# Edge lookups of a graph-attention router: a table of 116 rows and 27 blocks with a mask in twelve more rows, and one maximum in place of a product and a sum

## The chip, the cores and the metric

One core of one Trainium2 chip runs the whole program as a single launch. TensorE (PE in the profile), VectorE (DVE), ScalarE (ACT), GpSimd (POOL) and SyncE (SP, which here only issues DMAs) each run their own instruction stream and meet through semaphores. The metric is device time in microseconds from one launch; lower is better.

## The reference

The input is a graph with 3125 nodes of 256 features. The last of its stages, the only one whose main loop is touched, is a mixture of four experts whose router is a graph attention over 65536 edges and 4 heads:

```python
h = (x_flat @ W_gat).reshape(M, HEADS, NUM_EXPERTS)          # 4 heads x 4 experts
a_src = (h * att_src).sum(-1); a_dst = (h * att_dst).sum(-1)
e = leaky_relu(a_src[src] + a_dst[dst], negative_slope=0.2)
e_max = segment_max(e, dst); ee = exp(e - e_max[dst])
denom = segment_sum(ee, dst)
agg = segment_sum(h[src] * (ee / denom[dst])[:, :, None], dst)
scores = layernorm(agg + b_gat).mean over heads; w = softmax(top 2 of scores)
out = x + sum over experts ei of g[ei] * (gelu(x @ W1[ei] + b1[ei]) @ W2[ei] + b2[ei])
```

For each edge the kernel needs eight numbers of its destination node (two per head: a_dst less a bound, and 0.2 a_dst less the same bound) and twenty numbers of its source node.

## The kernel before, in words

The stage (`stage_router_and_experts`, tag `g1_`, F1 hidden columns) walks over 128 supertiles of 512 edges (GSUP = 128, SUP = 4 tiles of 128 edges), and beside them runs the experts: `program` spreads 4 experts x 5 groups of nodes x 6 steps = 120 steps over the first 120 supertiles, and the last 8 have edge work alone. All engines follow the order in which the code is written.

For supertile n the work is this.

- POOL gathers the twenty numbers of each edge's source by four indirect DMAs (`gather`, L2190), once DVE has copied their indices (`indices`, L2510).
- SP fetches the row numbers of the 512 edges, the same for every partition (`load_part`, L2659), and DVE compares them with the partition's own number (`turn_rows`, L2214): `turned_hot`, [125 rows, 512 edges], one-hot by row. The second instruction of `turn_rows` (L2217) makes `at_block`, a one-hot over 25 blocks for each edge.
- PE multiplies (`look_up`, L2753 and L2754) that one-hot with a table of 125 rows x 25 blocks x 8 numbers, cut in a high and a low part (`d_hi`, `d_lo`). What comes out in `found` (PSUM) is, for each edge, all 25 blocks of its row: 200 columns.
- DVE picks the block (`pick`): a product of the 800 numbers of a partition with `at_block` (L2524), a sum over the blocks (L2527), then three small instructions for the logit (L2531, L2532, L2535).
- ACT makes the weights (`weights`, L2806 and L2808, with two table loads) for two supertiles at once, and a one-hot over 261 places (`row_hots`, L2207 and L2210).
- DVE multiplies the weighted rows out over 12 classes (`scattered`, L2569, 1920 numbers), and PE adds them with 16 matmuls (L2735) into two PSUM banks.

DVE's order in supertile n is `weighted`, `classes`, `high`, `indices` for n + 4, `turned` for n + 3, `rest_of`, `pick` for n + 2, `scattered` for n. PE's order in step n is the sums of n with an expert's output (L2715, L2717) and one or two hidden tiles (L2197) between them, and `look_up` of n + 4. `look_up` of n + 4 waits for `turned` of n + 4 and for the reading of `found` by `pick` of n + 3 (semaphore `picked`); the sums wait for `spread_ready` and `hot_ready`.

At the stage's start DVE makes the table in place (`weigh_edges`, L2591 to L2595, semaphore `cut`), and PE begins with `pe.wait_ge(s["cut"], 5)`, `look_up(0, 0)`, hidden tiles, and three more lookups before step 0. The row and block numbers of the edges are worked out at the program's very start (`numbers` in `stage_open`), as work that DVE does between other work, and stored in DRAM by ACT (L1344). `gdst` is a DRAM tensor of 3125 x 8 that was used only in a branch for far-spread logits, which is not entered here.

## Time and profile before

| | |
|---|---|
| median of 3 runs | 4336.94 us (4331.12 to 4337.73) |
| profiled execution, its own time | 4339.91 us |
| its span | 4338.1 us |
| busy: PE, DVE, ACT, POOL | 3800.2, 2983.7, 2016.3, 2146.7 us |
| granted TensorE clock over the span | 0.871 of full speed |
| last stage | from about 3436 us to the end |

Times in views of the trace count from the span's start. An engine's busy time is the union of its instructions' durations. Matmuls are pipelined: each one's duration reaches over the start of the next, so the distance between two starts is what a matmul costs PE.

### The profile page before, as it was taken

Reading aid. Unit: us, or ns where it says so; the run is one execution under the profiler, and the core shown is the slowest. Engines: PE = TensorE matmul, PEld = TensorE weight load, DVE = VectorE, ACT = ScalarE, POOL = GpSimd, SP = SyncE. Lnnn points to the kernel's source line nnn. Section 1 sums busy time; section 2 is a strip of 40 time slices with the busy share of each in tenths; the row PEclk is TensorE's granted clock in tenths of the full one; section 3 lists DMA queues with packets and bytes.
Section 4 is the critical chain, followed back from the end, with each engine's and each line's share of the span. In section 5 each row is a group of like instructions: output and inputs, shape, how many; then the busy total and the mean of one; then the engine's idle time right before and its main releaser. Section 6 shows DMA issues by size and latency. Waiting matters only on the chain. (4 is left out here: it accounts for less than half of the span.)

```text
span 4338.1 us, 87724 instructions
## 1 busy us (share of the span) xinstructions
PE 3800.2 (88%) x23737; PEld 3412.1 (79%) x23737; DVE 2983.7 (69%) x6878; ACT 2016.3 (46%) x4710; POOL 2146.7 (49%) x2102
## 2 busy tenths in 40 slices
PE   7899999999999997997999677777777599999993
PEld 6799999999999986997887666666666578888883
DVE  7799999999999987555333222333332389999997
ACT  3566666666666655776222000000000278888871
POOL 0455555555555530000000777777777177777781
PEclk9999999999999997998999556666665599999996
DMA  4566666666666640002444333333333223333225
GB/s 132 148 175 178 176 176 177 175 178 176 175 178 175 178 122 18 19 14 65 160 150 151 110 105 105 104 104 105 105 104 105 57 59 78 69 77 73 62 51 122
DMA packets 226996, 509.04 MB, mean 117 GB/s; under 512 B 51806, under 2 KB 94300, under 8 KB 220427
## 3 DMA queue, kind: packets, MB, share of 16 engines
q0 software_dynamic: 116736, 313.66, 26.1%
q1 hardware_dynamic: 106389, 187.30, 15.5%
q10 hardware_dynamic: 3679, 5.79, 0.4%
q8 instruction: 89, 1.46, 0.1%
q14 instruction: 103, 0.84, 0.1%
HBM read 434.08 MB, written 72.49 MB: 117 GB/s over the span
## 5 line engine op out<-in xcount | busy, mean ns | idle before, releaser
L685 POOL DMA_INDIRECT big<-table,e_idx x784 | 747.1, 953 | 887.6 <-DVE e_idx L721 649.1
L356 POOL DMA_INDIRECT big<-table,e_idx x784 | 767.3, 979 | 819.6 <-DVE e_idx L460 353.5
L703 PE MATMUL psum<-e_near_hot,big 128*128 128x64 f32 x3136 | 604.0, 373 | 279.2 <-issue 200.6
L703 PEld LDWEIGHTS psum<-e_near_hot,big 128*128 128x128 f32 x3136 | 581.5, 284 | 312.4 <-issue 237.6
L2190 POOL DMA_INDIRECT g_S<-gsrc,g_idx x512 | 614.2, 1200 | 194.5 <-issue 158.9
L468 DVE TENSOR_TENSOR big<-psum,big 128x512 f32<-128x512 f32 x784 | 539.1, 688 | 36.9 <-PE psum L375 26.5
L435 ACT ACTIVATE e_hT_hi<-psum 128x256 fp32r<-128x256 f32 x784 | 300.7, 384 | 552.7 <-PE psum L375 552.7
L748 DVE TENSOR_TENSOR big<-big,psum 128x128 f32 x196 | 56.5, 288 | 662.9 <-PE psum L703 546.3
L386 PE MATMUL psum<-e_w_hi,e_hT_hi 128*128 128x256 f32 x1568 | 507.0, 323 | 0.3 <-ACT psum L420 0.3
L386 PE MATMUL psum<-e_w_hi,e_hT_lo 128*128 128x256 f32 x1568 | 442.1, 282 | 0.0
L386 PE MATMUL psum<-e_w_lo,e_hT_hi 128*128 128x256 f32 x1568 | 438.8, 280 | 0.0
L403 PE MATMUL psum<-e_near_hot,e_msg 128*128 128x64 f32 x3136 | 436.4, 262 | 0.2 <-DVE e_msg L506 0.2
L403 PEld LDWEIGHTS psum<-e_near_hot,e_msg 128*128 128x128 f32 x3136 | 411.7, 191 | 0.3 <-DVE e_msg L506 0.3
L2735 PE MATMUL psum<-g_hot,g_spread 128*120 128x262 f32 x2048 | 344.3, 305 | 42.6 <-DVE g_spread L2569 36.1
L506 DVE TENSOR_TENSOR e_msg<-psum,e_gate 128x256 f32<-128x256 f32 x784 | 331.0, 422 | 59.4 <-ACT e_gate L442 33.5
L223 ACT ACTIVATE e_t_low<-e_t_low 128x626 f32<-128x626 f32 (+1 forms) x10 | 7.2, 725 | 778.8 <-DVE e_t_low L232 778.8
L2735 PEld LDWEIGHTS psum<-g_hot,g_spread 128*120 128x120 f32 x2048 | 281.4, 187 | 67.4 <-issue 53.0
L481 DVE SCALAR_TENSOR_TENSOR e_hT_lo<-psum,e_hT_hi 128x256 fp32r<-128x256 f32 x784 | 324.6, 414 | 0.0
L442 ACT ACTIVATE e_gate<-big 128x256 f32<-128x256 f32 x784 | 318.8, 407 | 0.0
L367 PE MATMUL psum<-e_wb_hi,e_attr_parts 128*128 128x512 f32 x784 | 312.5, 399 | 2.5 <-DVE e_attr_parts L474 2.5
L368 PE MATMUL psum<-e_wb_lo,e_attr_parts 128*128 128x512 f32 x784 | 311.7, 398 | 0.0
L375 PEld LDWEIGHTS psum<-ident,big 128*128 128x128 f32 x1568 | 208.8, 141 | 128.1 <-issue 21.3
(395 smaller groups left out, 8942.5 us busy)
## 6 DMA issues: line engine op xcount, KB each, us to landing
big<-in_attr_t SPq DMA_DIRECT2D x392, 128.0 KB
g_rest<-gpart SPq DMA_DIRECT2D x128, 256.0 KB
big<-table,e_idx POOLq DMA_INDIRECT x1568, 2.8
table<-C SPq DMA_DIRECT2D x26, 896.0 KB
table<-n_rows SPq DMA_DIRECT2D x24, 896.0 KB
experts<-g_region SPq DMA_DIRECT2D x15, 560.0 KB
g_S<-gsrc,g_idx POOLq DMA_INDIRECT x512
table<-big SPq DMA_DIRECT2D x25, 224.0 KB
```

What stands on the lines that cost most here:

```text
L356: pool.indirect_dma_start(G[:, j % 2, q, :], None, table, bass.IndirectOffsetOnAxis(idx[:, j, q:q + 1], 0)).then_inc(s[f"G_in{j % 2}{q}"], 16)
L367: pe.matmul(c.ps[u % 2], tile, wb_hi[:, :], start=True, stop=False)
L386: last = pe.matmul(c.ps[4 + u % 2][:, 0:D], x, y[:, b, :], start=False, stop=b == KB - 1 and x is lo, skip_group_check=True)
L403: last = pe.matmul(acc[:, b, :], msg[:, u % 2, b * 128:(b + 1) * 128], hot, start=q == 0 and (b == 0 or s is sems[1]), stop=q == SUP - 1, ...
L442: act.activation(gate[:, u % SLOTS, :], Z[:, u % SLOTS, D:2 * D], ACT.Sigmoid).then_inc(s["gate_ready"], 1)
L468: dve.tensor_tensor(Z[:, u % SLOTS, :], c.ps[u % 2], G[:, j % 2, q, :], ALU.add).then_inc(s["zs_ready"], 1)
L481: dve.scalar_tensor_tensor(out=hT_lo[:, u % SLOTS, :, :].rearrange("p b n -> p (b n)"), in0=c.ps[2 + u % 2][:, 0:KB * 128], scalar=0.0, in ...
L506: dve.tensor_tensor(msg[:, u % 2, :], c.ps[4 + u % 2][:, 0:D], gate[:, u % SLOTS, :], ALU.mult).then_inc(s["msg_ready"], 1)
L685: pool.indirect_dma_start(G[:, j % n, q, :], None, c.table1, bass.IndirectOffsetOnAxis(idx[:, j, q:q + 1], 0)).then_inc(s[f"G_in{j % n}"], 16)
L703: last = pe.matmul(acc[:, b, :], G[:, j % n, q, b * 128:(b + 1) * 128], onehot[:, q, :], start=q == 0 and (b == 0 or s is sems[1]), stop=q ...
L2190: pool.indirect_dma_start(S[:, j, q, :], None, c.gsrc, bass.IndirectOffsetOnAxis(idx[:, j, 0, q:q + 1], 0)).then_inc(w_in[j], 16)
L2735: last = pe.matmul(sums[half], spread[:, j, 2 * u + p, half * CLASSES // 2:(half + 1) * CLASSES // 2, :].rearrange("p k c -> p (k c)"), ho ...
```

## The change

The table gets 116 rows and 27 blocks (116 x 27 = 3132), and twelve more rows: three for the tens digit of the block number to base 9, nine for its units digit. In these rows stands 0 for the blocks that have this digit, and -2^100 for those that don't. The one-hot gets 128 rows: the row number for partitions 0 to 115, the tens digit for 116 to 118, the units digit for 119 to 127. So in what PE gives out, every block but the edge's own is very negative, and DVE takes the maximum over the 27 blocks straight from PSUM. `at_block`, the product and one wait are gone. The table is brought into its new shape by a way through DRAM: rows_d to `gdst` and back into `table`. The constants `digit` and `off_block` are made in an earlier stage (`block_mask`, 12 small DVE instructions ahead of `stage_relations`' loop), the digits of the edges in `stage_open` (two more `divide`, two more stores by ACT).

```diff
+LP, LB, LOW = 116, 27, 9
+BIG = 2.0 ** 100
...
-                for out, made_here in ((c.gpart, at_row[:, 1, :]), (c.gnum[:, 0, :], block_of[:, 0, :]), (c.gnum[:, 1, :], at_row[:, 0, :]),
+                for out, made_here in ((c.gpart[0], at_row[:, 1, :]), (c.gpart[1], node[:, 1, :]), (c.gpart[2], block_of[:, 1, :]), (c.gnum[:, 0, :], block_of[:, 0, :]), (c.gnum[:, 1, :], at_row[:, 0, :]),
...
-                    yield from divide(block_of, at_row, node, TP)
+                    yield from divide(block_of[:, 0, :], at_row[:, 0, :], node[:, 0, :], TP)
+                    yield from divide(block_of[:, 1, :], at_row[:, 1, :], node[:, 1, :], LP)
+                    yield from divide(node[:, 1, :], block_of[:, 1, :], block_of[:, 1, :], LOW)
...
-        def turn_rows(dve, n, j):
-            dve.tensor_scalar(turned_hot[0:TP, j % 2, :], part_in[0:TP, j % 2, :], c.row[0:TP, :], None,
+        def turn_rows(dve, j):
+            dve.tensor_scalar(turned_hot[:, j % 2, :], part_in[:, j % 2, :], c.digit[:, :], None,
                               ALU.is_equal).then_inc(s["turned_ready"], 1)
-            c.fence(dve)
-            dve.tensor_tensor(at_block[:, j, :, :], bc(c.iota[:, 0:NT], 1, SUP),
-                              bc(lo[:, bass.ds(n * SUP, SUP)], 2, NT), ALU.is_equal).then_inc(s["block_ready"], 1)
+        PART_ROWS = ((0, LP), (LP, LP + LB // LOW), (LP + LB // LOW, 128))
...
                 dve.wait_ge(s["looked_up"], n + 1 + 2)
-                dve.wait_ge(s["block_ready"], n + 1)
-                dve.tensor_tensor(chosen_rows, found[:, :, 0:NT * 2 * GH].rearrange("p q (c t) -> p q c t", t=NT),
-                                  bc(at_block[:, j, :, :], 2, 2 * GH), ALU.mult).then_inc(s["picked"], 1)
+                dve.tensor_reduce(picked[:, j % 2, :, :], found[:, :, 0:LB * 2 * GH].rearrange("p q (c t) -> p q c t", t=LB), AX.X,
+                                  ALU.max).then_inc(s["picked"], 1)
+                x, above, below = w[:, j % 2, :, :], picked[:, j % 2, :, 0:GH], picked[:, j % 2, :, GH:2 * GH]
                 dve.wait_ge(s["picked"], n + 1)
-                dve.tensor_reduce(picked[:, j % 2, :, :], chosen_rows, AX.X, ALU.add).then_inc(s["e_steps"], 1)
...
+            dve.wait_ge(table_in, 32)
+            cut(dve.tensor_tensor(by_column, by_column, bc(c.off_block[:, :], 1, 2 * GH), ALU.add))
             cut(dve.tensor_copy(high_part, by_column))
             cut(dve.tensor_tensor(low_part, by_column, high_part.bitcast(F32), ALU.subtract))
...
             def load_part(n, j):
                 if not (isinstance(n, int) and n < 2):
                     sp.wait_ge(s["turned_ready"], n - 1)
-                c.fence(sp)
-                sp.dma_start(part_in[:, j, :], c.gpart[bass.ds(n, 1), :].broadcast_to([128, SUP * 128])).then_inc(
-                    s[f"part_in{j}"], 16)
+                for kind, (a, b) in enumerate(PART_ROWS):
+                    c.fence(sp)
+                    sp.dma_start(part_in[a:b, j, :], c.gpart[kind, bass.ds(n, 1), :].broadcast_to([b - a, SUP * 128])).then_inc(
+                        s[f"part_in{j}"], 16)
...
+            sp.wait_ge(s["cut"], 3)
+            for a, b in ROWS:
+                sp.dma_start(gdst_v[a:b], rows_d[a:b, :, :]).then_inc(table_out, 16)
+            sp.wait_ge(table_out, 32)
+            sp.wait_ge(cleared, 1)
+            whole = LP * (LB - 1)
+            sp.dma_start(table[0:LP, 0:LB - 1, :], c.gdst[0:whole].rearrange("(t p) d -> p t d", p=LP)).then_inc(table_in, 16)
+            sp.dma_start(table[0:NODES - whole, LB - 1, :], c.gdst[whole:NODES]).then_inc(table_in, 16)
             for n in (2, 3, 4):
                 load_part(n, n % 2)
...
-                    out = found[:, q, 0:NT * 2 * GH]
-                    hot = turned_hot[0:TP, j, q * 128:(q + 1) * 128]
+                    out = found[:, q, 0:LB * 2 * GH]
+                    hot = turned_hot[:, j, q * 128:(q + 1) * 128]
...
-            pe.wait_ge(s["cut"], 5)
+            pe.wait_ge(s["cut"], 6)
             look_up(0, 0)
```

DVE's instructions in one supertile of the loop, from the second one-hot (L2217, written to `g_region`, where at_block lies) to the last step of `pick`; before (ISA and REGISTER_ALU rows are waits and register steps):

```order
L2217 TENSOR_TENSOR g_region<-iota,g_rest 128x100
L2553 ISA
L2554 TENSOR_TENSOR g_parts<-g_R,g_parts 128x4x20
L2522 REGISTER_ALU
L2524 TENSOR_TENSOR g_chosen_rows<-psum,g_region 128x800
L2527 TENSOR_REDUCE g_picked<-g_chosen_rows 128x32
L2529 ISA
L2530 ISA
L2531 TENSOR_TENSOR g_w<-g_S,g_picked 128x16
L2532 SCALAR_TENSOR_TENSOR g_picked<-g_S,g_picked 128x4x4
L2534 REGISTER_ALU
L2535 TENSOR_TENSOR g_w<-g_w,g_picked 128x16
```

And of the change, the same place, from the row one-hot (L2240) on, which before stood two rows ahead of L2217:

```order
L2240 TENSOR_SCALAR g_turned_hot<-g_rest,digit 128x512
L2577 ISA
L2578 TENSOR_TENSOR g_parts<-g_R,g_parts 128x4x20
L2549 REGISTER_ALU
L2550 TENSOR_REDUCE g_picked<-psum 128x32
L2553 REGISTER_ALU
L2554 ISA
L2555 TENSOR_TENSOR g_w<-g_S,g_picked 128x16
L2556 SCALAR_TENSOR_TENSOR g_picked<-g_S,g_picked 128x4x4
L2558 ISA
L2559 TENSOR_TENSOR g_w<-g_w,g_picked 128x16
```

Two instructions are gone, and the reduction now reads PSUM itself, and is what frees it.

SP's instructions at the start of the stage's main block, of the change (`g_rest` holds part_in, 512 row numbers for each partition; before, only one issue of 128x512 stood here for each supertile):

```order
L2716 DMA gdst<-g_rows_d 112x25x8
L2716 DMA gdst<-g_rows_d 13x25x8
L2720 DMA g_table<-gdst 116x26x8
L2721 DMA g_table<-gdst 109x8
L2686 DMA g_rest<-gpart 116x512
L2686 DMA g_rest<-gpart 3x512
L2686 DMA g_rest<-gpart 9x512
```

The four table DMAs stand ahead of the first row loads, the second two wait for the first two, and DVE's `table_in` and with it PE's first lookup wait behind them.

## Rows read from the trace of the kernel before

**Rows 1.** Page: span; part 1, busy time of each engine.

```profile
span 4338.1 us, 87724 instructions
...
PE 3800.2 (88%) x23737; PEld 3412.1 (79%) x23737; DVE 2983.7 (69%) x6878; ACT 2016.3 (46%) x4710; POOL 2146.7 (49%) x2102
```

**Rows 2.** Windows: length, busy time of PE, PEld, DVE, ACT, POOL, clock, DMA.

```profile
3496.00:4187.00 691.00, 668.91 (x4187) 592.27 (x4187) 663.70 (x1473) 587.75 (x1041) 545.47 (x451) 1.00 0.31 69
4187.00:4266.00 79.00, 57.67 (x349) 52.73 (x348) 69.23 (x149) 42.47 (x82) 46.92 (x39) 0.85 0.51 104
```

**Rows 3.** Source view of L2569: duration min/median/max, first and last start.

```profile
L2569 DVE TENSOR_TENSOR g_spread<-g_at_class,g_parts x128: 2157/2158/2200, 3489.0 to 4260.9; 128x1920 fp32r<-128x1920 f32 x128
```

**Rows 4.** Groups by line, 3500 to 4180 us: busy, mean of one, idle before.

```profile
L2190 POOL DMA_INDIRECT g_S<-gsrc,g_idx x445 | 538.3, 1210 | 143.7 <-issue 139.8 <-DVE g_idx L2510 3.9
L2735 PE MATMUL psum<-g_hot,g_spread 128*120 128x262 f32 x1780 | 296.9, 302 | 21.6 <-DVE g_spread L2569 16.2 <-issue 4.1
L2569 DVE TENSOR_TENSOR g_spread<-g_at_class,g_parts 128x1920 fp32r<-128x1920 f32 x112 | 241.7, 2158 | 2.1
...
L2527 DVE TENSOR_REDUCE g_picked<-g_chosen_rows 128x32 f32<-128x800 f32 x112 | 110.4, 986 | 3.9
L2524 DVE TENSOR_TENSOR g_chosen_rows<-psum,g_region 128x800 f32<-128x800 f32 x111 | 108.5, 977 | 0.0
```

**Rows 5.** Waits of PE, 3490 to 4187 us: total, times, longest.

```profile
PE psum L2735 <- DVE g_spread L2569: 19.4, 26, 2.7
```

**Rows 6.** Timeline of DVE in one supertile: start, length.

```profile
3803.33 0.24 DVE L2217 TENSOR_TENSOR g_region<-iota,g_rest 128x100 f32<-128x100 f32 x1
3803.50 0.24 DVE L2554 TENSOR_TENSOR g_parts<-g_R,g_parts 128x80 fp32r<-128x80 f32 x1
3803.66 0.98 DVE L2524 TENSOR_TENSOR g_chosen_rows<-psum,g_region 128x800 f32<-128x800 f32 x1
3804.67 0.99 DVE L2527 TENSOR_REDUCE g_picked<-g_chosen_rows 128x32 f32<-128x800 f32 x1
3805.80 0.17 DVE L2531 TENSOR_TENSOR g_w<-g_S,g_picked 128x16 f32<-128x16 f32 x1
```

**Rows 7.** Timeline of PE, two lookup matmuls.

```profile
3801.52 0.27 PE L2753 MATMUL psum<-g_d_hi,g_turned_hot 125*128 125x200 f32 x1
3801.63 0.27 PE L2754 MATMUL psum<-g_d_lo,g_turned_hot 125*128 125x200 f32 x1
```

**Rows 8.** Timelines of SP and POOL, 3436 to 3462 us.

```profile
3438.44 10.16 SPq L2230 DMA_DIRECT2D gsrc<-g_rows_s  x2
...
3454.89 0.96 POOL L2190 DMA_INDIRECT g_S<-gsrc,g_idx  x1 [18.06 <-DMA gsrc<-g_rows_s]
```

**Rows 9.** DMA queues, 3444.8 to 3453.3 us: packets, MB, share of 16 engines.

```profile
q1 hardware_dynamic: 3225, 0.36, 39.5%
```

**Rows 10.** DMA issues, 3436 to 3462 us: KB, median us to landing.

```profile
g_src_i<-gint SPq DMA_DIRECT2D x1, 256.0 KB, 3.1
```

**Rows 11.** Timeline of DVE at the stage's start.

```profile
3467.45 0.26 DVE L2593 COPY g_rows_d<-g_x 125x100 f32<-125x100 f32 x1
3467.75 0.34 DVE L2594 CAST g_d_hi<-g_rows_d 125x200 fp32r<-125x200 f32 x1
```

**Rows 12.** Timeline of ACT at the end of the first stage's loop.

```profile
98.95 1.47 ACTq L1344 DMA_DIRECT2D gnum<-big  x3
```

**Rows 13.** Timeline of PE behind it.

```profile
103.88 23.40 PE L1536 MATMUL psum<-big 125*128 125x257 f32 x100 [2.23 <-ACT big L1347]
```

**Rows 14.** Groups by line, 0 to 140 us: a reduction from PSUM.

```profile
L1440 DVE TENSOR_REDUCE o_top<-psum 128x2 f32<-128x250 f32 x1 | 0.4, 418 | 0.5 <-PE psum L1524 0.5
```

**Rows 15.** Timeline, 2390 to 2400 us: first matmuls of the relations.

```profile
2398.99 1.30 PE L703 MATMUL psum<-e_near_hot,big 128*128 128x64 f32 x5 [11.38 <-DMA big<-table,e_idx]
```

**Rows 16.** Timelines of SP and DVE, last supertiles.

```profile
4230.60 21.30 SPq L2697 DMA_DIRECT2D g_region<-experts  x4
...
4254.22 0.18 DVE L2531 TENSOR_TENSOR g_w<-g_S,g_picked 128x16 f32<-128x16 f32 x1 [3.89 <-DMA g_S<-gsrc,g_idx]
```

More of the change, by code:

```diff
@@ L771, in dve_pass @@
                     do(dve.tensor_scalar(wide_iota[:, part * 128:(part + 1) * 128], c.iota[:, :], float(part * 128), None, ALU.add))
+                block_mask(do)
             def aside(dve, w, g, h, sup):
@@ L778, in dve_pass, with block_mask @@
             (loop_beside(step, -lead, aside) if s is sems[0] else loop(step, -lead))(dve)
+        def block_mask(do):
+            dve = do.eng
+            high_row, low_row, tens, units, differs = mask_work[:, 0:1], mask_work[:, 1:2], *(
+                mask_work[:, 2 + n * LB:2 + (n + 1) * LB] for n in range(3))
+            block = c.iota[:, 0:LB]
+            do(dve.tensor_scalar(high_row, c.row[:, :], float(LP), None, ALU.is_ge))
+            do(dve.tensor_scalar(low_row, c.row[:, :], float(LP + LB // LOW), None, ALU.is_ge))
+            do(dve.scalar_tensor_tensor(out=c.digit[:, :], in0=high_row, scalar=-float(LP), in1=c.row[:, :], op0=ALU.mult, op1=ALU.add))
+            do(dve.scalar_tensor_tensor(out=c.digit[:, :], in0=low_row, scalar=-float(LB // LOW), in1=c.digit[:, :], op0=ALU.mult,
+                                        op1=ALU.add))
+            do(dve.tensor_tensor(high_row, high_row, low_row, ALU.subtract))
+            do(dve.tensor_scalar(tens, block, float(LOW), None, ALU.is_ge))
+            do(dve.scalar_tensor_tensor(out=tens, in0=block, scalar=float(2 * LOW), in1=tens, op0=ALU.is_ge, op1=ALU.add))
+            do(dve.scalar_tensor_tensor(out=units, in0=tens, scalar=-float(LOW), in1=block, op0=ALU.mult, op1=ALU.add))
+            do(dve.tensor_scalar(differs, tens, c.digit[:, 0:1], high_row, ALU.not_equal, ALU.mult))
+            do(dve.tensor_scalar(units, units, c.digit[:, 0:1], low_row, ALU.not_equal, ALU.mult))
+            do(dve.tensor_tensor(units, units, differs, ALU.add))
+            do(dve.tensor_scalar(c.off_block[:, :], units, -BIG, None, ALU.mult))
         def both(eng, one):
@@ L1362, in divide @@
                     def divide(out, left, x, by):
-                        yield dve.tensor_scalar(out, x, 1.0 / by, -(by // 2) / by, ALU.mult, ALU.add)
+                        yield dve.tensor_scalar(out, x, 1.0 / by, -(by - 1) / (2 * by), ALU.mult, ALU.add)
                         yield dve.tensor_scalar(out, out, WHOLE, None, ALU.add)
@@ L2111, in stage_router_and_experts @@
         turned_hot = sb("turned_hot", [128, 2, SUP * 128], F32R)
-        d_hi, d_lo = sb("d_hi", [TP, NT * 2 * GH], F32R), sb("d_lo", [TP, NT * 2 * GH], F32R)
+        d_hi, d_lo = sb("d_hi", [128, LB * 2 * GH], F32R), sb("d_lo", [128, LB * 2 * GH], F32R)
+        table = sb("table", [128, LB, 2 * GH])
         st = sb("st", [TP, 4, NT])
@@ L2157, in stage_router_and_experts @@
         a_src, a_dst, m_dst = rows_s[:, :, 0:GH], rows_d[:, :, 0:GH], rows_d[:, :, GH:2 * GH]
-        names = ("below_zero", "idx_ready", "begun", "cut", "part_in0", "part_in1", "turned_ready", "block_ready", "looked_up",
+        names = ("below_zero", "idx_ready", "begun", "cut", "part_in0", "part_in1", "turned_ready", "looked_up",
                  "picked", "e_steps", "e_ready", "w_ready", "R_ready", "spread_ready", "off_ready", "hot_ready",
@@ L2175, in load_w2 @@
             sp.dma_start(w2[:, :, :], by_block(c.i["m1_w2"][bass.ds(e, 1)])).then_inc(w2_in, 16)
-        numbered, b2_in, b2_cut, two_made, dst_in = (
-            c.sem(tag + n) for n in ("numbered", "b2_in", "b2_cut", "two_made", "dst_in"))
+        numbered, b2_in, b2_cut, two_made, dst_in, cleared, table_out, table_in = (
+            c.sem(tag + n) for n in ("numbered", "b2_in", "b2_cut", "two_made", "dst_in", "cleared", "table_out", "table_in"))
         loaded, steps, ends_ready, turned_ends, diag_ready, all_ready, rows_ready, rows_in = (
@@ L2273, in _ @@
                 do(dve.tensor_copy(far_i[:, :], far[:, 1:2]))
+                dve.memset(table[:, :, :], 0.0).then_inc(cleared, 1)
                 for n in range(2):
-                    dve.wait_ge(s[f"part_in{n}"], 16)
-                    turn_rows(dve, n, n)
+                    dve.wait_ge(s[f"part_in{n}"], 48)
+                    turn_rows(dve, n)
                 dve.wait_ge(b2_cut, 1)
@@ L2505, in weigh_edges @@
         def weigh_edges(dve):
-            STEPS_E = 3
+            STEPS_E = 2
             def indices(k, j):
@@ L2585, in supertile @@
                 scattered(k, j)
-            by_column = rows_d[:, :, :].rearrange("p t c -> p c t")
-            high_part, low_part = (a[:, :].rearrange("p (c t) -> p c t", t=NT) for a in (d_hi, d_lo))
+            by_column = table[:, :, :].rearrange("p t c -> p c t")
+            high_part, low_part = (a[:, :].rearrange("p (c t) -> p c t", t=LB) for a in (d_hi, d_lo))
             cut = Chain(dve, s["cut"])
```

23 lines of the change are left out of this document (11 added, 12 removed).

## The prediction

> **What bounds the kernel now.** The page first: the span is 4338.1 us, PE is busy for 88% of it and DVE for 69% [rows 1]. The profiled execution took 4339.91 us, 1.8 us above its span and 3.0 above the median of the runs shown (4336.94), so I work out a difference in the span and take it from the median. A time within 0.2% (8.7 us) of the median can't be told from no change by a measurement of this kernel.
>
> The change sits in the last stage, so I cut that out in windows [rows 2]. From 3496 to 4187 us the clock is at its full level (1.00 granted) and two engines are nearly full: PE 668.9 of 691 us, DVE 663.7. ACT has 587.8, POOL 545.5. Shares do not say which of the two sets the pace; the chain of waits does. The last instruction of a supertile on DVE (L2569) runs 128 times from 3489.0 to 4260.9 us: 771.9 / 127 = 6.08 us for each supertile [rows 3]. In the waits of PE in that stretch one releaser stands out: DVE's spread, 26 times, 19.4 us [rows 5]. On DVE one instruction follows the other (3803.33, 3803.50, 3803.66, 3804.67, 3805.80) with no wait marked [rows 6]. So DVE sets the pace, but PE stands close behind. PE's idle time there is 691 - 668.9 = 22.1 us. A wait shows too short, since a matmul of L2735 has a duration of 302 ns [rows 4] where starts lie about 120 ns apart: 28 waits hide about 0.18 us each, 5 us. PE could save 27 us of 691, which is 114 supertiles: it needs (691 - 27) / 114 = **5.82 us each**. From 4187 us on there is little expert work: PE is busy for 57.7 of 79 us [rows 2], and DVE alone decides.
>
> **What the change takes off DVE.** The block one-hot L2217: 3803.33 to the next start at 3803.50, 0.17 us. The product L2524: 3803.66 to 3804.67, 1.01 us with its wait [rows 6]. The reduction grows from 800 to 864 numbers. At 800 it takes 986 ns [rows 4]; a spread of 1920 takes 2158, so a number costs (2158 - 986) / 1120 = 1.05 ns, and 64 of them 0.07 us. That it reads PSUM costs nothing visible: 250 numbers reduced from PSUM took 418 ns [rows 14], and 986 - 550 x 1.05 = 409 is what 250 from SBUF would be. DVE saves 0.17 + 1.01 - 0.07 = **1.11 us per supertile** and needs 4.97. The upper bound of the reduction is twice the price per number (0.9 us more), if 216 PSUM columns in runs of 27 read badly; the PSUM row and L2524 (977 ns for 800 from PSUM) speak against it.
>
> **What PE, ACT and POOL then allow.** PE's lookups have 216 columns for 200. Two starts in a lookup are 0.11 us apart [rows 7]; L2735, with 262 columns, about 0.12. The 16 columns cost between nothing and 16 / 200 x 0.11 = 9 ns, over 8 x 114 matmuls 0 to 8 us. I take 0, as the two distances hardly differ for 62 columns. ACT's busy time is 587.8 / 114 = 5.16 us per supertile, POOL's 545.5 / 114 = 4.8 (a gather 1.21 [rows 4], four of them 4.84 to 5.0). Both lie under 5.82. So in the first 114 supertiles PE is the next bound, and of the 1.11 us only 0.24 can be had. Of the 27 us I take 22: ACT is 0.66 us short of PE on average, but unevenly (the weights of two supertiles come in one of them, with two table loads), so some waits for `hot` stay. Bounds 12 and 27. **-22 us.**
>
> From 4187 us on DVE's saving counts in full until the transfers decide. SP's last loads of expert outputs begin at 4230.60, and at 4254.22 DVE waits 3.89 us for the last gather, which lands among them [rows 16]. These loads begin once `turned` has run in supertile 122, and the landing follows them, so what counts is the saving up to there: 9 or 10 supertiles x 1.11. What is saved behind turns into a longer wait for that gather. Bounds 6 and 14. **-11 us.** In the lead-in DVE's first spread stands behind one pick: **-1 us.**
>
> **What it adds.** The way of the table through DRAM. DVE must have made the third cut (L2593, ends 3467.7), then come a store of 3125 pieces of 32 bytes, its landing, a load of 3016 pieces and one of 109, their landing, an addition, and only then the high part that now begins at 3467.75 [rows 11]. All PE work of the block is written behind `cut`, even the hidden tiles, and ACT and DVE hang on PE: nothing covers this way. No such load is in the trace. The nearest row is the store of rows_s with the same 3125 pieces (of 80 bytes): issued at 3438.44, POOL's first gather waits for it until 3454.89 [rows 8], 16.4 us. Part of that is queueing behind four other loads: between 3444.8 and 3453.3 us its queue moved 3225 packets in 8.5 us while another queue shared the engines [rows 9]. The smallest DMA of the stage landed in 3.1 us [rows 10]. The packets took 39.5% of 16 engines for 8.5 us, 53.7 us for 3225, 16.7 ns each. So a transfer is at best 3.1 + 3125 x 16.7 ns / 16 = 6.4 us, two in series 12.7; at worst each is as slow as that store, 33 us. I take **20 us**, nearer to the lower end, since at 3467 us only POOL's gathers and the row loads run beside. The addition is one more instruction of the size of L2594 (0.34 us) [rows 11]: **+0.4**.
>
> The row loads become three issues for each supertile (about 0.35 us each on SP, which has nothing else to do) with the same bytes; a row block is asked for two supertiles before it is compared, some 11 us, against a landing of 3.1: 0. If the cover goes, each supertile loses what the loads are longer than that.
>
> In the first stage ACT issues two more stores before its table load and 25 exponentials; three such issues take 1.47 us [rows 12], so its first exponential comes 1.0 us later. PE's L1536 begins on that exponential and then runs without a gap for 23.4 us [rows 13]: **+1.0**. The eight more DVE instructions there are half as long as those replaced and go into slots where DVE has time beside PE. The 12 instructions of `block_mask`, some 2.4 us, delay the first one-hot of the relations from 2392 to 2395 us, but PE's first matmul there waits for a gather until 2398.99 [rows 15]: 0; without this cover 2.4 us.
>
> **Sum.** -22 - 11 - 1 + 20 + 0.4 + 1.0 = -12.6 us, a span of 4325.5; from the median, 4336.9 - 12.6 = **4324 us**.
>
> **Rivals.**
> - *The load uses few DMA engines.* The trace does not show on how many engines a DMA of 116 partitions runs. If it is a quarter of them, the 3016 pieces take four times as long: at 16.7 ns a piece 12.6 us in place of 3.1, the way 24 us and the time 4328; at the pace of the store (8.5 us for 3125 packets) 4 x 8.2 = 33 us, the way about 3.1 + 8.5 + 3.1 + 33 = 48, and the time 4324 + 28 = 4352: slower. It decides from 33 us on, where all gains are spent. For it: 116 is divisible by 4 and not by 8 or 16, and the code splits other transfers of 125 rows in 112 and 13. Against: 3125 pieces went through in 8.5 us with the engines shared. 0.17 for the slow end.
> - The Trainium skill, "DMA: Bandwidth & Descriptors", section "Why a DMA increments its semaphore by 16 and not by 1", says that a DMA spreads over the largest number up to 16 that divides its slowest dimension: 4 for 116 partitions, and 1 for 109. By that rule and the two prices above the way through DRAM is 24 to 48 us; no row here shows it directly.
> - *PE or ACT keep their stalls.* The waits for the spread become waits for `hot` or for gelu's banks, and only the end gains: -5 - 11 - 1 + 21.4 = +4, 4341. For it: ACT's small reserve. Against: ACT's busy 5.16 against 5.82. 0.2.
> - *PE is no limit*, its busy time being an artefact of modelled ends: 123 supertiles x 1.11 = 137 us less, 4337 - 137 + 20 = 4220. Against: matmul starts follow each other without gaps for most of a step. 0.02.
> - *The reduction reads PSUM at half pace*, and DVE keeps 5.9 us: 4337 - 2 x 11 + 21 = 4336 with PE a little better fed. 0.06.
> - The forecast as worked out: 0.55.
>
> **Range and chances.** The likeliest case with its bounds: -27 - 14 - 1 + 12.7 + 1.4 = -28, 4309, to -12 - 6 + 33 + 1.4 = +16, 4353; not all bad ends meet, and 8 in 10 lie between 4307 and 4346. Faster by over 0.2% (under 4328.3) 0.55: most of the forecast and the small case of 137 us; the same 0.27; slower (over 4345.6) 0.18.
>
> **What would show it.** The spread (L2593 in the change) at 5.85 us on average from its 5th to 115th start, with DVE's waits on PE or ACT in place of PE's on DVE; DVE's reduction at about 1.06 us; lookup starts still 0.11 apart; PE's first lookup about 20 us later after the block's start; the relations unchanged; PE's L1536 1 us later. The prediction is wrong if the two table transfers take over 33 us together, if PE idles over 15 us more in the 114 supertiles than the 5 left to it, or if a reduction over PSUM takes 1.5 us.

## The result and the profile after

The changed kernel takes **4381.7 us** (median of 5 runs, 4377.4 to 4388.3) against 4336.9 for the kernel before: 1.0103 times as long, 95% interval 1.0089 to 1.0116. It is slower by 45 us, where 4324 was forecast and 4307 to 4346 given as the range. The span of the profiled execution grew from 4338.1 to 4380.6 us. The page, part 1, answers to [rows 1]:

```profile
span 4380.6 us, 87715 instructions
...
PE 3810.1 (87%) x23737; PEld 3424.1 (78%) x23737; DVE 2848.3 (65%) x6644; ACT 2016.5 (46%) x4710; POOL 2181.3 (50%) x2102
```

DVE is busy for 135 us less, as the change wants, and POOL, of which the change says nothing, for 35 us more. The source view of the spread and the groups by line from 3510 to 4190 us answer to [rows 3] and [rows 4]:

```profile
L2593 DVE TENSOR_TENSOR g_spread<-g_at_class,g_parts x128: 2157/2159/2228, 3503.3 to 4301.4; 128x1920 fp32r<-128x1920 f32 x128
```

```profile
L2216 POOL DMA_INDIRECT g_S<-gsrc,g_idx x430 | 551.1, 1282 | 131.0 <-issue 128.9 <-DVE g_idx L2537 2.1
...
L2770 PE MATMUL psum<-g_hot,g_spread 128*120 128x262 f32 x1736 | 285.6, 303 | 33.5 <-DVE g_spread L2593 33.5
...
L2550 DVE TENSOR_REDUCE g_picked<-psum 128x32 f32<-128x864 f32 x108 | 113.2, 1048 | 12.5 <-PE psum L2789 12.5
...
L2584 DVE TENSOR_TENSOR g_R<-g_S,g_R 128x64 f32<-128x64 f32 x108 | 23.9, 221 | 51.8 <-ACT g_R L2843 51.8
...
L2555 DVE TENSOR_TENSOR g_w<-g_S,g_picked 128x16 f32<-128x16 f32 x108 | 20.0, 186 | 94.4 <-DMA g_S<-gsrc,g_idx 86.0 <-DVE g_picked L2550 0.2
```

In the last of these fences the columns are busy time, mean duration in ns, and the idle time before with what ended it. The reduction costs 1048 ns, what was forecast. But DVE now waits 86 us for gathers, a wait that the kernel before did not have, and 51.8 us for ACT's weights (5 before), and PE waits longer for DVE's spread (33.5 us). The window that answers to the first of [rows 2]:

```profile
3510.00:4201.00 691.00, 653.97 (x4052) 581.13 (x4051) 521.67 (x1209) 566.41 (x1005) 558.13 (x437) 0.98 0.33 68
```

PE's busy time fell from 668.9 to 654.0, DVE's from 663.7 to 521.7; POOL's rose from 545.5 to 558.1. The granted TensorE clock is 0.98 for 1.00, which is worth some 0.1 us of PE's time per supertile. The 42.5 us of span lie in three places:

- before the first spread: 3503.3 for 3489.0, **+14.3** (by DVE's instructions 0.6 ahead of the stage, 4.7 in its opening block, 34.3 us for 29.6, and 9.0 in the main block up to the first spread);
- the loop, 127 distances: 798.1 for 771.9, **+26.2**: 6.28 us per supertile for 6.08. From the 5th to the 115th start, where 5.85 was forecast, it is 6.30 for 6.10;
- from the last spread to the end: 79.2 for 77.2, **+2**.

**The way through DRAM** was shorter than forecast. Timeline of SP and DVE in `after`:

```profile
3473.05 1.94 SPq L2716 DMA_DIRECT2D gdst<-g_rows_d  x2
...
3477.21 0.24 SPq L2720 DMA_DIRECT2D g_table<-gdst  x1
...
3477.51 4.71 SPq L2721 DMA_DIRECT2D g_table<-gdst  x1
...
3484.00 0.54 DVE L2619 TENSOR_TENSOR g_table<-g_table,off_block 128x216 f32<-128x216 f32 x1 [10.98 <-DMA g_table<-gdst]
```

DVE waits 10.98 us; from the third cut to the addition it is 11, not 20, and the load took most of it (3477.2 to 3484.0).

**POOL.** Its timeline shows where the loop's time went:

```profile
3803.62 0.95 POOL L2216 DMA_INDIRECT g_S<-gsrc,g_idx  x1 [0.31 <-issue]
3804.87 0.94 POOL L2216 DMA_INDIRECT g_S<-gsrc,g_idx  x1 [0.30 <-issue]
3806.12 0.94 POOL L2216 DMA_INDIRECT g_S<-gsrc,g_idx  x1 [0.30 <-issue]
3807.37 2.39 POOL L2216 DMA_INDIRECT g_S<-gsrc,g_idx  x1 [0.30 <-issue]
```

and of DVE beside it:

```profile
3806.30 0.18 DVE L2555 TENSOR_TENSOR g_w<-g_S,g_picked 128x16 f32<-128x16 f32 x1 [4.12 <-DMA g_S<-gsrc,g_idx]
...
3806.79 2.16 DVE L2593 TENSOR_TENSOR g_spread<-g_at_class,g_parts 128x1920 fp32r<-128x1920 f32 x1
3808.86 0.22 DVE L2584 TENSOR_TENSOR g_R<-g_S,g_R 128x64 f32<-128x64 f32 x1
```

A gather takes 0.94 us, and 0.30 us lie between two: 1.25 each, 5.0 for four. But the one that begins at 3807.37, inside the spread, takes 2.39 us: it ends at 3809.76, 0.81 us behind the spread's end (3808.95). That is no accident: of 106 gathers that begin from 3520 to 4180 us and take longer than 1 us, 104 began in a spread, and their ends lie 0.80 to 0.83 us behind its end. In the kernel before it is the same (109 of 110). Those that begin in the first 0.04 us of a spread are not held (5 in the changed kernel). Gathers that begin in the reduction are not held either (103 in L2527 before, 41 in L2550 after: all under 0.96 us). So POOL needs 5.0 us and what the spread holds it: 1.05 us for each held gather before, 1.30 after. By the group rows, (busy + idle) / count x 4: before (538.3 + 143.7) / 445 x 4 = **6.13** [rows 4], after (551.1 + 131.0) / 430 x 4 = **6.35**. This quotient is the window's length divided by its supertiles and would come out for any engine; it is POOL's need because only 3.9 and 2.1 us of the idle time were waits for another engine. POOL was not at 4.8 of 6.08, it ran without a pause in both kernels.

The Trainium skill, "SBUF — State Buffer", section "Who interferes with whom", says that a DVE instruction with two SBUF inputs contends with a GpSimd instruction that reads SBUF, which its second input's read interface is shared with. The trace agrees so far: the spread has two SBUF inputs, the reduction has one or none, and a gather reads its list of rows from SBUF. The same section also says that a `tensor_tensor` was seen not to stall DMAs, and infers that making their descriptors needs the write interface only; the 104 gathers here were held by a `tensor_tensor`, and for gathers the measurement decides.

The size of the hold could be read before: a gather takes 1.21 us on average [rows 4] and 0.96 where no DVE work is beside it [rows 8], so four of them lose 1.0 us.

So theory A is: POOL's gathers, held by the spread, set the pace. Rival B: the row loads of 116 partitions go over few DMA engines and make the gathers land late. The DMA queues from 3520 to 4180 us speak for it: the gathers' packets (q0) took 9.9% of the 16 engines before and 15.2% after, with nearly the same bytes.

```profile
q0 software_dynamic: 13795, 4.44, 9.9%
```

```profile
q0 software_dynamic: 13337, 4.29, 15.2%
```

### The profile page after: what moved, and what is told of

The parts are those of the page before. It is cut to its first block and busy times, and to the rows that moved or that the text cites. A ratio compares the mean times of both kernels' runs of the same rounds, so it can differ in the third digit from the quotient of the medians.

```text
span 4380.6 us, 87715 instructions
## 1 busy us (share of the span) xinstructions
PE 3810.1 (87%) x23737; PEld 3424.1 (78%) x23737; DVE 2848.3 (65%) x6644; ACT 2016.5 (46%) x4710; POOL 2181.3 (50%) x2102
## 5 line engine op out<-in xcount | busy, mean ns | idle before, releaser
L2216 POOL DMA_INDIRECT g_S<-gsrc,g_idx x512 | 649.0, 1268 | 200.4 <-issue 152.7
```

Source lines behind the costliest of these rows:

```text
L2216: pool.indirect_dma_start(S[:, j, q, :], None, c.gsrc, bass.IndirectOffsetOnAxis(idx[:, j, 0, q:q + 1], 0)).then_inc(w_in[j], 16)
```

## The experiments

The runs fell on five chips. On three of them the kernel before took 4339 to 4341 us (e1 to e8, e17, e18). On the other two it took 4554 and 4626 (e9 to e12, e13 to e16). Ratios are to the kernel before on the same chip. The changed kernel was not run again beside e1 to e8, e17 and e18. Its 4381.7 us stand beside 4336.9 for the kernel before, 2 to 4 us less than beside those, so where a difference to it is small, go by the ratios and the traces.

**e1: the changed kernel, transfers of 116 partitions cut in 112 and 4.**

```
-        PART_ROWS = ((0, LP), (LP, LP + LB // LOW), (LP + LB // LOW, 128))
+        PART_ROWS = ((0, 0, 112), (0, 112, LP), (1, LP, LP + LB // LOW), (2, LP + LB // LOW, 128))
...
-            sp.dma_start(table[0:LP, 0:LB - 1, :], ...)
+            for a, b in ((0, 112), (112, LP)):
+                sp.dma_start(table[a:b, 0:LB - 1, :], ...[a:b])
```

> The changed kernel, with each transfer of 116 partitions cut into one of 112 and one of 4: the row loads of every supertile (now four for three) and the load of the table. Theory A (the pace of the last stage is set by POOL's gathers, which DVE's spread holds up): the spread still comes every 6.28 us, within 0.05; only the way of the table gets shorter, since 3016 pieces landed over 6 us with few engines, so the time is 1 to 5 us under the changed kernel's 4381.7, about 4378. Rival B (the row loads go over few DMA engines and hold up the gathers' landings): the spread falls to 6.1 or below, and the time is 20 us or more shorter, about 4358.

Measured: 4357.7 us, ratio 1.0041 (1.0027 to 1.0055), 24 us less than the change (27 by the two ratios). The spread stands from 3500.6 to 4280.5 us, 6.14 per supertile; the queue row went back:

```profile
q0 software_dynamic: 13626, 4.39, 10.2%
```

Rival B has its share: 18.2 us of the loop. But 6.14 is still over what DVE or PE need, and POOL's group gives (547.3 + 133.9) / 439 x 4 = 6.21:

```profile
L2216 POOL DMA_INDIRECT g_S<-gsrc,g_idx x439 | 547.3, 1247 | 133.9 <-issue 130.8 <-DVE g_idx L2537 3.1
```

The gain comes by way of POOL: the mean gather is 1247 ns for 1282 and the idle time for each is the same (0.305 us), and 4 x 35 ns x 127 = 18 us. That later landings move the spread to where it holds a gather longer is argued from this, not shown.

DVE's wait for the addition of the table fell to 8.30 us from 10.98.

**e2 and e3: three of four gathers, in the changed kernel and in the one before.**

```
-            for q in range(SUP):
+            for q in range(SUP if isinstance(k, int) and k == 0 else SUP - 1):
                 pool.indirect_dma_start(S[:, j, q, :], None, c.gsrc, ...)
```

> The changed kernel with three of the four gathers of each supertile; the fourth quarter of the edges keeps the rows of the first four supertiles, so part of the result is left out. Row loads, DVE, PE and ACT do what they did. Theory A: POOL needs 3 x 1.245 = 3.74 us and what the spread holds it, under 5; the pace falls to PE's 5.82, at most 5.95, so 127 x 0.33 to 0.46 = 42 to 58 us off 4381.7: 4324 to 4340. Rival B (row loads): the pace stays over 6.1 and the time over 4358, since the row loads are the same.

> The kernel before with three of the four gathers, with the same part of the result left out. It gives what DVE alone allows there. Theory A: DVE's own work decides, 6.08 less what POOL held it up, 5.95 to 6.05 per supertile; time 4321 to 4333. Against the changed kernel with three gathers this tells what the change is worth once POOL is not the bound: by the prediction's own sum about 12 us in favour of the change, less the 13 us that the opening block and lead-in took more than before. If POOL had nothing to do with the pace before, the time is unchanged at 4337.

Measured: 4305.7 (0.9921, 0.9908 to 0.9935) and 4329.7 (0.9978, 0.9969 to 0.9987). The source views of the spread, of e2 and then of e3:

```profile
L2593 DVE TENSOR_TENSOR g_spread<-g_at_class,g_parts x128: 2144/2158/2169, 3499.8 to 4228.4; 128x1920 fp32r<-128x1920 f32 x128
```

```profile
L2569 DVE TENSOR_TENSOR g_spread<-g_at_class,g_parts x128: 2157/2180/2230, 3488.7 to 4250.4; 128x1920 fp32r<-128x1920 f32 x128
```

That is 728.6 / 127 = 5.74 us and 761.7 / 127 = 6.00. With POOL out of the way the change takes **33 us** off the loop, which is what the prediction had worked out (22 + 11): 23.1 up to the 115th spread and 9.9 from there to the last. The changed kernel is 24 us faster than the one before with the same three gathers (21 between the profiled executions), better than the forecast of 12.6. The row loads of e2 are those of the changed kernel, so with POOL relieved they cost little; between e4 and e8 below it is 5 us.

**e4 and e5: the spread in four instructions, in the changed kernel and in the one before.**

```
+                each = 2 * SUP // 4
+                for a in range(0, 2 * SUP, each):
+                    piece = dve.tensor_tensor(spread[:, j % 2, a:a + each, :, :], bc(at_class[:, j % 2, a:a + each, :], 3, CH),
+                                              bc(parts[:, j % 2, a:a + each, :].bitcast(F32), 2, CLASSES), ALU.mult)
+                piece.then_inc(s["spread_ready"], 1)
```

> The changed kernel with the spread of 1920 numbers a partition as four instructions of 480, one for each quarter of the edges, one behind the other. Each costs DVE a start of about 0.1 us more, so DVE needs 0.3 us more per supertile (5.3 for 4.97). Theory A in the form that a gather can't begin or end while one instruction of DVE reads two operands from SBUF, but can between two: POOL is held less, the pace falls to 5.85 to 6.1 and the time to 4327 to 4360. If the hold is by the port over the whole stretch, with no gap that a gather can use, the pace stays at 6.28 to 6.4 and the time at 4380 to 4395. Rival B: no change but DVE's 0.3 us, which is hidden: 4382.

> The kernel before with its spread as four instructions of 480 numbers. In the changed kernel one such instruction took 652 ns, four 2.61 us for 2.16: 0.45 us more of DVE per supertile. With three gathers the kernel before ran at 6.00 us per supertile, DVE's own need. Theory A (before: DVE sets the pace and POOL stands close behind; after: POOL): here DVE is the bound, so the pace rises to 6.00 + 0.45 = 6.45 and the time by 127 x 0.37 = 47 us, to about 4385, though POOL is held less. If POOL were the bound of the kernel before too, the time would fall as it did in the changed kernel, to 4320 or less.

Measured: 4318.0 (0.9951, 0.9938 to 0.9965), 64 us less than the change and faster than before; and 4357.4 (1.0034, 1.0023 to 1.0046), slower. The same edit helps where POOL is the bound and hurts where DVE is. The loop takes 738 us for 798. A gather is now held by one piece only: those that begin 1.01 to 1.03 us behind the spread's start, in its second piece, end at 2.05, 0.82 us behind that piece's end and 0.3 ahead of the whole spread's. The price on DVE was less than expected: four pieces take 2.36 us for 2.16, not 2.61, as the next one starts while one drains; so e5 rose by 17 us and not by 47. POOL's group in e4, (477.7 + 203.2) / 465 x 4 = 5.86, has 75 us of waiting for DVE in it, so that POOL has a reserve again:

```profile
L2216 POOL DMA_INDIRECT g_S<-gsrc,g_idx x465 | 477.7, 1027 | 203.2 <-issue 127.9 <-DVE g_idx L2537 75.3
```

**e6: the kernel before with its row load cut in 116, 3 and 9 partitions.**

```
-                sp.dma_start(part_in[:, j, :], c.gpart[bass.ds(n, 1), :].broadcast_to([128, SUP * 128])) ...
+                for a, b in ((0, 116), (116, 119), (119, 128)):
+                    sp.dma_start(part_in[a:b, j, :], c.gpart[bass.ds(n, 1), :].broadcast_to([b - a, SUP * 128])) ...
```

> The kernel before with nothing of the change but the cut of each row load in 116, 3 and 9 partitions (the same rows and bytes). Theory B as the first experiment leaves it: a load of 116 partitions goes over few DMA engines, packets of the gathers take some 230 ns for 143 and land later. With DVE close to its own bound here this costs less than in the changed kernel, where it was 24 us: 5 to 24 us, 4345 to 4364. If only POOL's hold matters, or the loads only cost where POOL sets the pace: 4340 within 4.

Measured: 4344.2 (1.0008, 0.9999 to 1.0017). The loop is unchanged (3492.1 to 4263.5, 6.07 per supertile), though the gathers' packets took longer just as in the changed kernel:

```profile
q0 software_dynamic: 13824, 4.45, 16.7%
```

So this costs nothing in a loop whose DVE does not wait for gathers. (The row gives 0.167 x 16 x 660 us / 13824 = 128 ns for a packet, and 76 in the kernel before; the 230 and 143 ns of the expectation stand in no row.)

What e6 does lengthen is the opening block, 33.2 us for 29.6, which is most of what the change adds there (34.3). SP's issue of the source rows' store shows it, in the changed kernel, in e6 and in e8 below (10.16 us before, [rows 8]):

```profile
3440.44 14.46 SPq L2256 DMA_DIRECT2D gsrc<-g_rows_s  x2
```

```profile
3439.84 15.16 SPq L2233 DMA_DIRECT2D gsrc<-g_rows_s  x2
```

```profile
3445.55 9.96 SPq L2273 DMA_DIRECT2D gsrc<-g_rows_s  x2
```

In e8 eight row loads stand ahead of the store in place of two, but none of 116 partitions, and its opening block takes 29.6 us (29.4 in e17). So it is the loads of 116 partitions that cost there, not the number of issues.

The Trainium skill, "DMA: Bandwidth & Descriptors", section "Why a DMA increments its semaphore by 16 and not by 1", gives, by its rule of the largest divisor up to 16, 4 engines for 116 partitions; the q0 rows and e1 agree that the load of 116 burdens a few engines and one of 112 does not. That section was quoted ahead for the table's load alone; the row loads, by it, are the larger case.

**e7: the table's way through DRAM in the opening block.**

```
+        def cut_table(do):
+            do(do.eng.tensor_tensor(cut_rows[:, :, 0:GH], a_dst, m_dst, ALU.subtract))
+            do(do.eng.scalar_tensor_tensor(out=cut_rows[:, :, GH:2 * GH], in0=a_dst, scalar=0.2, in1=m_dst, ...))
...
                 leaky(do, dve, m_dst, x4[:, :, :])
+                cut_table(do)
```

> The changed kernel with the first two cuts written to a tile of their own in the opening block, and the way of the table through DRAM begun there (with its load in 112, 4 and 109 partitions), so that it runs beside the store of the source rows and the first gathers. The loop is unchanged. If the way through DRAM is worth what its place in the trace says (DVE waits 10.98 us for it, and three small cuts of about 0.2 to 0.3 us go): 9 to 12 us less than 4381.7, about 4371. If the block's head waits for something else next (part loads, POOL, PE), less than 5.

Measured: 4368.8 (1.0069, 1.0056 to 1.0083), 0.34% or 15 us less than the change by the two ratios. From the main block's first DVE instruction to the first spread it is 18.9 us (3464.39 to 3483.3) for 31.9, and the loop's pace is the change's own, 6.28. The way through DRAM with its three cuts cost some 13 us, all of it on the path, and can be hidden.

**e8: spread in four, 112 and 4 partitions, early table**, the three edits above together.

> The changed kernel with the spread in four, all transfers of 116 partitions in 112 and 4, and the early table. Spread in four gave 4318. The early table takes off 9 to 12. The loads over more engines: with POOL no longer the bound, PE sets the pace at 5.74 to 5.79, so they give 0 to 5 in the loop. Sum 4301 to 4309, about 4306. If the loads still cost what they did in the first experiment (24 us), 4285 to 4290.

Measured: 4305.1 (0.9918, 0.9905 to 0.9932), 77 us less than the change and 36 less than before. From e4 it is 14 us by the ratios. The two traces put more than e7's share there: from DVE's first instruction of the stage to the end it is 860.4 us for 881.4. Of these 21 us 5.1 lie in the opening block and 11.0 between it and the first spread; 5.4 lie in the loop (732.5 us for 737.9, and 733.2 in e17), so the wider loads still give 5 us there, the top of the 0 to 5 expected. The window from 3500 to 4180 us has PE at 675.4 of 680:

```profile
3500.00:4180.00 680.00, 675.43 (x4307) 606.00 (x4306) 582.61 (x1641) 598.26 (x1070) 482.02 (x468) 1.00 0.34 72
```

**e9 to e12, on a chip with 4554 us for the kernel before.** e9 reads the spread from one tile (the products with the edges' rows are left out), e10 has the spread in two, e11 does the reduction twice, e12 is e8 with SP's store of the source rows ahead of the first row loads.

```
e9   dve.tensor_scalar(spread[...], bc(at_class[:, j % 2, :, :], 3, CH), 1.0, None, ALU.mult)
e10  each = 2 * SUP // 2
e11  dve.tensor_reduce(picked[:, j % 2, :, :], ...).then_inc(s["padded"], 1); dve.wait_ge(s["padded"], n + 1); the same again
```

> The changed kernel with its spread read from one tile alone: the class one-hots times 1.0, as a tensor_scalar of the same 1920 numbers a partition, so the products with the rows of the edges are left out. It is as long an instruction on DVE in the same place (1 number a cycle: 1.9 to 2.2 us). Theory A with the port as its cause (a gather reads its list from SBUF through what DVE needs for a second SBUF operand): no gather is held, none of them takes over 1.05 us, the pace is PE's 5.74 to 5.80 and the time 4308 to 4320. If any long instruction of DVE holds a gather: 6.2 to 6.3 and 4375 to 4385.

> The changed kernel with the spread as two instructions of 960 numbers. The pace was 6.28 with one and 5.79 with four. Theory A: a gather is held for at most half as long, but another may be held by the second half; POOL loses 0.4 to 0.9 us a supertile for 1.33, so 5.8 to 5.95, and the time is 4320 to 4340.

> The changed kernel with its reduction from PSUM done twice (the same result twice), with a wait between: 1.1 us more of DVE per supertile, what the change had saved. Theory A in its full form (POOL is held by the spread, and how long hangs on where its gathers stand to it; DVE with little to spare falls into step so that the spread begins just behind a gather's start): the pace is that of the kernel before, 6.08 to 6.17, so the kernel with more work is faster than without it: 4355 to 4368. If POOL is a bound of 6.28 whatever DVE does: 4380 to 4385. If DVE's work simply adds: 4400 and more.

> The kernel of e8 with SP's store of the source rows written ahead of its eight first row loads in the opening block. There the store was issued only behind those issues, and POOL's first gather waited for it. If the store sets when POOL begins and POOL sets when DVE's first spread starts: 2 to 6 us less than 4305. If the tables and PE's first work decide the head: 4305 within 3.

Measured: 4699.7 (1.0319), 4718.9 (1.0347), 4605.9 (1.0115) and 4749.0 (1.0432). None of the expected times can be read there: everything is slow on that chip, already in the relations (1488 matmuls of PE between 2500 and 3000 us in e12, 1756 in the kernel before on the first chips). e9, e10 and e12 take 7.2 to 7.6 us per supertile, though e12 is e8 but for one edit; e11 is the fastest with 6.42. What can be read is what does not hang on PE. e12's opening block takes 27.3 us for the 29.6 and 29.4 of e8 and e17, so the store ahead of the row loads gives 2 us. And in e10 a gather begun in one half of the spread ends 0.82 us behind that half's end. **e13 to e16**, the changed kernel itself with e9, e10 and e11 beside it, fell on a chip with 4626:

> The changed kernel as it is, beside the three that follow, on one chip. Theory A and rivals alike: 1.010 times the kernel before, the spread every 6.28 us, if the chip is like the first ones. On a chip like the last one (before: 4554), where the clock falls again and again in the last stage: not known.

> The kernel of e9 once more: the spread read from one tile alone. There it took DVE 1.16 us, not 2.16, and gathers that began in it took 1.48 us for 0.94, so they were held even with one SBUF operand; an instruction that fast reads through both ports for one operand. Theory A with a shared port: a hold of at most 1.0 us, POOL needs 5.0 + 0.2 to 0.6, the pace is PE's 5.74 to 5.80, and the time 0.980 to 0.987 of the changed kernel's beside it.

> The kernel of e10 once more: the spread in two instructions. Theory A: a held gather loses at most half as much, the pace is 5.8 to 5.95, the time 0.985 to 0.990 of the changed kernel's beside it. If the hold hangs on the whole stretch: 1.00.

> The kernel of e11 once more: the changed kernel with 1.1 us more of DVE per supertile. Theory A in its full form: DVE with little to spare stays in step with POOL's gathers so that its spread begins just before one of them, as in the kernel before; pace 6.08 to 6.17, time 0.994 to 0.997 of the changed kernel's beside it, with more work. If POOL is a bound of 6.28 whatever DVE does: 1.000 to 1.001. If DVE's work adds: over 1.005.

Measured: 4651.0 (1.0058), 4735.7 (1.0235), 4751.3 (1.0280) and 4681.5 (1.0111). The three stand in the same order again. This is the only place where the changed kernel ran beside e16, its own padded form, and there the padded one is slower, by 0.5% (6.99 us per supertile for 6.64); so e16's expectation came out wrong there, and that more work can be faster is shown only for chips on which the kernel before takes 4340 us (e18 below). What the traces of e9 and e14 do show is a gather's hold. Timelines of POOL and of DVE in e9:

```profile
3805.03 1.75 POOL L2216 DMA_INDIRECT g_S<-gsrc,g_idx  x1 [0.30 <-issue]
```

```profile
3804.80 1.16 DVE L2593 TENSOR_SCALAR g_spread<-g_at_class 128x1920 fp32r<-128x1920 f32 x1 [0.47 <-PE psum L2770]
```

With one input the same 1920 numbers take 1.16 us for 2.16, and the gather that begins at 3805.03 ends at 3806.78, 0.82 us behind the spread's end (3805.96). So the experiment didn't take the hold away: the faster form of the instruction holds POOL too. In e9 the gathers that begin up to 0.5 us ahead of it are held as well (all 42 between 3750 and 4450 us), and end 0.12 us behind its end. That two inputs from SBUF are the cause is not shown by it. What speaks for them is that the reductions, with one input from SBUF or none, hold nothing, and neither does the product of PSUM and one SBUF tile (L2524, 0.98 us; in e3 107 gathers begin in it, none over 0.95 us).

**e17 and e18: e8's kernel and e11's once more**, on a chip with 4338.9 for the kernel before.

> The kernel of e8 as it was (0.992 of the kernel before there, a spread's first piece every 5.75 us). If the chip made e12 slow: on a chip with 4340 for the kernel before, 4305 again; on one with 4550 or more, 1.03 to 1.05 times the kernel before, with a granted clock of 0.90 to 0.95 in the loop. If e12's own edit did it: 0.992 on either.

> The changed kernel with 1.1 us more of DVE per supertile. On a chip with 4340 for the kernel before: by theory A in its full form pace 6.08 to 6.17 and 4355 to 4368, less than the 4382 without the padding; if POOL is a bound of 6.28 whatever DVE does, 4380 to 4385; if DVE's work adds, 4400 and more. On one with 4550 or more it came out at 1.011 twice and tells nothing new.

Measured: e17 4302.3 (0.9919, 0.9906 to 0.9933), what e8 gave. **e18 4355.7 (1.0040, 1.0026 to 1.0054): 1.1 us more work on DVE in each supertile, and the kernel is 0.6%, 27 us by the two ratios, faster than the change on its chip.** Source view of its spread and POOL's group:

```profile
L2596 DVE TENSOR_TENSOR g_spread<-g_at_class,g_parts x128: 2144/2158/2227, 3508.1 to 4276.8; 128x1920 fp32r<-128x1920 f32 x128
```

```profile
L2216 POOL DMA_INDIRECT g_S<-gsrc,g_idx x446 | 537.7, 1206 | 147.4 <-issue 135.0 <-DVE g_idx L2537 12.4
```

The pace is 768.7 / 127 = 6.05, the mean gather 1206 ns as before the change (1210), for 1282. In e18 92 of the gathers that begin near a spread begin 0.1 to 0.3 us ahead of it, so the next begins 1.0 to 1.2 into it and is held for about 1 us; in the changed kernel the held gathers begin anywhere from 0.1 to 1.3 us into it, and are held for 1.3 us. So the phase between the two engines sets the length of the hold. Why it settles so is argued only: where DVE is nearly the bound, it would fall in step with POOL; where it waits for a landing (34 of 108 supertiles in the changed kernel), its spread starts 0.5 us behind it, wherever POOL's next gather then is.

## Why the prediction was wrong

- **The step that failed:** "ACT's busy time is 587.8 / 114 = 5.16 us per supertile, POOL's 545.5 / 114 = 4.8 (a gather 1.21 [rows 4], four of them 4.84 to 5.0). Both lie under 5.82." For POOL it is wrong. The row that it rests on [rows 4] has 143.7 us of idle time beside the 538.3 of busy time, 139.8 of it "issue", which means that POOL waited for nothing: 1.21 + 0.32 = 1.53 us a gather, 6.13 for four. POOL stood at the loop's pace already, so there was next to nothing for a saving on DVE to gain. Its busy time was no need either: a gather takes 0.94 us alone, and the rest of the 1.21 is the hold by DVE's spread.
- **DVE's saving, 1.11 us:** the reduction came out at 1048 ns (1.06 forecast). e11's form with the work put back runs at 6.05 (e18), near the pace before.
- **PE's bound, 5.82 and 22 us:** up to the 115th spread 5.86 measured with POOL relieved (e2), 5.82 in e8. The 22 us are 23.1 in e2 against e3. Right, and not to be had with POOL as it is.
- **"The row loads ... 0":** wrong in the changed kernel, 18 us of the loop (e1). What was not looked at is what they do to the gathers on the same engines. In the loop of the kernel before they cost nothing (e6).
- **The way through DRAM, +20:** 11 in the trace, below the lower bound of 12.7, and 13 by e7. The rival of few engines was right that the load of 116 partitions is burdened, but its 24 to 48 us did not come: cutting it gave 2.7 us (e1). It missed that the row loads were the larger part. By its own prices its first case is 22 us, not 24 (12.7 - 3.1 + 12.6).
- **Left out:** the opening block, 4.7 us longer. POOL's first gather goes from 3454.89 [rows 8] to 3458.7. e6 has 3.6 us of it by three row loads for one, and e8 and e17 have none of it with 112 and 4 partitions, so it is again the loads of 116.
- **The supertiles from the 115th on, -11:** 81.4 us for 76.4 up to the last spread, +5.0, as POOL's gathers set these too; with POOL relieved -9.9 (e2 against e3). Behind the last spread +2.
- **The rivals:** none had POOL. "PE or ACT keep their stalls" describes part of what one sees, at a fifth of the chance, but with another cause and 4341.
- **The sums:** rows 5 have 26 waits where the working takes 28, and the upper end leaves out the 1 us of the lead-in; neither changes the forecast.

Sum by the runs: -33 (the change on DVE) + 18 (loads over few engines) + 41 (POOL's gathers with their hold: the fourth one costs 779.9 - 728.6 = 51 us in e1's loop over e2's, and cost 771.9 - 761.7 = 10 before) + 14 (ahead of the first spread) + 2 = 42 us. The first three are differences of the same five loops and so must add up to its 26 us; that it is the hold and not the number of gathers is shown by e4, which makes all of them and takes 60 us off the loop.

What stays open: why the phase in the changed kernel settles where it does, and what slows dense kernels on the two slow chips. The granted clock is part of it. Windows of the loop, e17 and then e12 (e8 but for one edit):

```profile
3500.00:4200.00 700.00, 688.34 (x4388) 617.84 (x4387) 599.90 (x1687) 609.76 (x1092) 496.06 (x482) 1.00 0.33 75
```

```profile
3750.00:4450.00 700.00, 588.11 (x3281) 499.83 (x3282) 444.00 (x1247) 457.45 (x816) 355.82 (x357) 0.93 0.26 57
```

The clock stays at its 2.4 GHz level in e17, and drops to 1.2 GHz for some of the time in e12 (0.50 from 3903 to 3908 us, 0.93 on average). At a mean of 0.93 e17's 5.77 us per supertile would be 5.77 / 0.93 = 6.2; it is 7.58, with waits of ACT whose releaser the profile can't name (153 us in this window). This was not tried further.

## What to carry to other kernels

Before an engine is called free, add to its busy time the idle time that the profile puts down to "issue" (not its waits for others), and divide by the count: a gather of 0.94 us came every 1.53. Look at the longest of such instructions and at what runs on the other engines when they are long; an instruction held by a neighbour looks busy, and its length moves with the phase between the two. When DVE and POOL both stand near the pace, cut the long DVE instruction into pieces before you shorten DVE's work, and cut partition counts that few DMA engines share into 112 and the rest.

## What the runs showed of the hardware

- A gather (indirect DMA by POOL) that begins in a DVE multiplication of two SBUF tiles ends 0.82 us behind that instruction's end, in the median, whatever that one's length (2.16, 1.16 or 0.65 us); one that begins up to 0.3 us ahead of it or in its first 0.04 us is not held.
- The same hold comes from a one-input tensor_scalar of 1920 numbers that runs in 1.16 us, there also for gathers that begin up to 0.5 us ahead of it, which end 0.12 us behind it; reductions of 0.99 and 1.05 us hold nothing, nor does a product of PSUM and SBUF of 0.98 us.
- Four DVE instructions of 480 numbers in a row take 2.36 us, one of 1920 takes 2.16: 0.07 us for each cut.
- Loads of 116 partitions raised the engine share of other packets from 9.9 to 15.2%; of 112 and 4 it is 10.2%. Ahead of a store of 3125 rows they raised its issue on SP from 10.2 to 14.5 and 15.2 us; with 112 and 4 it was 10.0 and 10.8.
- The same kernel took 4339 to 4341 us on three chips, 4554 and 4626 on two, and there the order of kernels was another (e8's kernel 0.992 of the kernel before, e12's, its near twin, 1.043).
